# The FFN's bias as a matmul of three bf16 rows, in place of additions on GpSimd

## The chip, the cores and the metric

One core of a Trainium2 chip runs the whole program. The time is the device time of one execution in microseconds. The engines work side by side and wait for each other by semaphores: TensorE (PE, with PEld for its weight loads), VectorE (DVE), ScalarE (ACT), GpSimd (POOL) and SyncE (SP), which issues the DMAs.

## What is computed

x is 4 batches of 2048 rows of 256 values. The kernel computes a "macaron" block: half an FFN, attention, half an FFN.

```
ffn(x) = x @ W.T + b + (x @ V_r) @ C.T          # b: 256 values, V_r and C: rank 32
x = x + 0.5 * ffn(layernorm(x))
x = x + attn(layernorm(x))                      # 16 heads of 16, causal, polymax in place of softmax
x = x + 0.5 * ffn(layernorm(x))
```

`polymax` is x*x + 1 for positive scores and a straight line for negative ones, over 1000. The two FFNs have the same weights and the same bias.

## The kernel before

The 8192 rows are cut into 16 chunks of 512 (a chunk is 4 blocks of 128 rows). Each chunk goes through three stages: A (LayerNorm `ln1`, transposes `z1T`, first FFN `ffn`, LayerNorm `ln2`, transposes `z2T`), B (q, k, v, their splits into three bf16 parts, and a running state) and C (projection `proj`, LayerNorm `ln3`, transposes `z3T`, second FFN `out`). W and V_r C are folded into one matrix `w_ffn` at the start, already times 0.5.

Between them runs the attention, 16 iterations (4 batches by 4 groups of 4 heads) of 40 tiles, each tile in two halves. A half is two heads' scores: bf16 matmuls into the PSUM tile `score`, of which there are two. DVE or ACT raises them into `rp` (`L926`, `L831`); on tiles of the diagonal a mask is applied on POOL (`L710`) and a linear part `lin` is made; POOL and ACT square them (`L735`, `L847`, `L851`), and PE multiplies by v into `y_ps` three tiles later.

The order is written out by hand. A global list of slots says what every engine does; each engine walks the same slots in its own queue. A whole iteration has 80 slots, one half in each. The tables `A_FULL`, `B_FULL`, `C_FULL` put the stages' jobs into the slots: in a whole iteration `ffn` has slots 38 to 45 of a chunk's A stage, `out` slots 71 to 78 of another chunk's C stage. A job fills one of two PSUM banks (`bank`) in pieces, one piece a slot. A job of `ffn` or `out` has 4 pieces: two blocks of rows, and for each the two halves (`kc`) of the 256 inputs. Its chunk has two such jobs.

Every matmul is cut by `strips` into four of 32 columns of its stationary operand. They go to the four column groups of the array, run side by side, and are called a set below. An fp32 matmul leaves two records in the trace, a bf16 one leaves one. So a piece of `ffn` is 8 records of `bank<-w_ffn,zT`, and a set of scores is 4 records of `score<-qs,ks`.

The bias is added on POOL: `add_bias` runs in four slots behind the four of `normalise`, in place on the FFN's input x (`x_sb` for `ln1`, the tile `x2`, shown as `x`, for `ln3`), and its last part raises `xb_ready` or `x2b_ready`. DVE waits for that before it empties a bank with x = x + bank (`L897` for `ffn`, `L908` for `out`). DVE and POOL take everything in the order of their queues, so what stands behind a waiting instruction waits too.

Of the kernel before, what the change touches and what calls it, by code (L numbers as in the profile page):

```python
# [7 lines left out]
BF16 = mybir.dt.bfloat16  # L8
ALU = mybir.AluOpType
# [3 lines left out]
P = 128  # L13
BATCH, SEQ, DM = 4, 2048, 256
HEADS, HD = 16, 16
KC = DM // P
CH = 512
NB = CH // P
# [6 lines left out]
STRIP = 32  # L25
# [4 lines left out]
SPLITS = 3  # L30
# [83 lines left out]
C_LATE = {"proj": (0, 4), "ln3": 8, "z3T": (20, 21), "out": (22, 26)}  # L114
C_SHORT = {"proj": (0, 4), "ln3": 8, "z3T": (20, 21), "out": (22, 26)}

AGGR, SCALES, ROOT, NORM, BIAS = NB, NB + 4, NB + 2, NB + 5, 2 * NB + 5


@dataclass(eq=False)  # L120
# [17 lines left out]
class Order:  # L138
# [27 lines left out]
    def finish(self):  # L166
        self.jobs.sort(key=lambda x: x.start)
        ends = [x.start + PIECES[x.kind] for x in self.jobs]
        assert ends == sorted(ends)
        per = {"act": 0, "dve": 0}  # L170
        for k, x in enumerate(self.jobs):
            per[x.who] += 1
            x.k, x.emptied = k, per[x.who]
        self.place = {(x.kind, x.chunk, x.i): x for x in self.jobs}
        self.pieces, self.empties, self.steps = {}, {}, {}
        for x in self.jobs:
            for p in range(PIECES[x.kind]):
                self.pieces.setdefault(x.start + p, []).append((x, p))
            self.empties.setdefault(x.empty_at, []).append(x)
        for (kind, chunk), at in self.ln.items():  # L180
            for step in range(BIAS + NB):
                self.steps.setdefault(at + step, []).append((kind, chunk, step))

    def made(self, kind, chunk, i):
# [96 lines left out]
def build(nc, x_in, w_attn, w_proj, ffn_w, ffn_b, ffn_v, ffn_c, out):  # L281
    ctx = ExitStack()
    with ctx:
        def sb(name, shape, dt=F32):
            return ctx.enter_context(nc.sbuf_tensor(name, shape, dt))
# [4 lines left out]
        def sem(name):  # L290
            return ctx.enter_context(nc.semaphore(name))
# [14 lines left out]
        w_qkv = sb("w_qkv", [P, KC, 3 * DM])  # L306
        w_out = sb("w_out", [P, KC, DM])
        bias_half = sb("bias_half", [P, DM])
        smask = sb("smask", [QR, DM])
        slope_mask = sb("slope_mask", [P, 2, P])  # L310
        rise = sb("rise", [P, 1])
# [62 lines left out]
        x1_stored = sem("x1_stored")  # L374
# [3 lines left out]
        st_stored = sem("st_stored")  # L378
        c_loaded = sem("c_loaded")
        out_stored = sem("out_stored")  # L380
        xb_ready = sem("xb_ready")
        x2b_ready = sem("x2b_ready")
        stats_done = {k: sem(f"stats_{k}") for k in LNS}
        aggr_done = {k: sem(f"aggr_{k}") for k in LNS}
        var_done = {k: sem(f"var_done_{k}") for k in LNS}
# [3 lines left out]
        z_ready = {k: sem(f"z_ready_{k}") for k in LNS}  # L389
# [266 lines left out]
        def _(pool):  # L656
# [26 lines left out]
            pool.wait_ge(const_ready, 14)  # L683
            pool.tensor_scalar(bias_half[:], bias_half[:], 0.5, 0.0, ALU.mult, ALU.add).then_inc(const_ready, 1)
            pool.wait_ge(const_ready, CONSTS)

            def normalise(k, src, dst, chunk, i):
                if i == 0:
# [9 lines left out]
                                         ALU.mult, ALU.add)  # L698
                if i == NB - 1:
                    ins.then_inc(z_ready[k], 1)  # L700

            def add_bias(k, x, ready, chunk, i):
                if i == 0:
                    pool.wait_ge(z_ready[k], chunk + 1)
                ins = pool.tensor_tensor(x[:, i, :], x[:, i, :], bias_half[:], ALU.add)
                if i == NB - 1:
                    ins.then_inc(ready, 1)

            def mask(block, heads_in_it, fill=0.0):
                pool.affine_select(out=block, in_=block, compare_op=ALU.is_ge, fill=fill, base=0,  # L710
# [4 lines left out]
            def slot(s):  # L715
                H = o.halves.get(s)
                if H is not None and H % 2:
                    T = H // 2
                    off = TILES[T % NT][2]
                    buf = rp[T % RP_BUFS]  # L720
                    if is_diag(T) and shared(T):
                        wait_raised(pool, H)
                        mask(buf[:, 2:4, off:off + P], 2, -RISE)
                        wait_lin(pool, H)
                        mask(lin[diag_index(T) % L_BUFS][:, 2:4, :], 2)
                        wait_raised(pool, H - 1)
                        mask(buf[:, 0:2, off:off + P], 2)
                        pool.wait_ge(masked, o.masked[T] + 3)
                    elif is_diag(T):
                        wait_raised(pool, H)  # L730
                        mask(buf[:, :, off:off + P], QH)
                    if shared(T):
                        wait_raised(pool, H - 1)
                        half = buf[:, 0:2, off:CH]
                        pool.tensor_tensor(half, half, half, ALU.mult).then_inc(squared["pool"], 1)  # L735
                for k, chunk, step in o.steps.get(s, ()):
                    src, dst = {"ln1": (x_sb, z), "ln2": (x1, z), "ln3": (x2[chunk % 2], z3)}[k]
                    if 0 <= step - NORM < NB:
                        normalise(k, src, dst, chunk, step - NORM)
                    if 0 <= step - BIAS < NB and k != "ln2":  # L740
                        add_bias(k, src, xb_ready if k == "ln1" else x2b_ready, chunk, step - BIAS)
                for b, i, step in split_at.get(s, ()):
                    if b >= EARLY and step != 1:
                        split(pool, b, i, step)
                for x in o.empties.get(s - 1, ()):
                    if x.kind == "state":
                        b, i = x.chunk, x.i
                        wait_emptied(pool, "state", b, i)
                        if i == 0 and b > 0:
                            pool.wait_ge(st_stored, b * 16)  # L750
                        if i > 0 or b % CPB:
                            pool.wait_ge(st_added, b * NB + i)
                        add = st_add[i % 2][:].rearrange("r (h d) -> r h d", h=HEADS)
                        if i == 0 and b % CPB == 0:
                            if b == 0:
                                pool.wait_ge(st_zero, 16 * BATCH)
                            pool.tensor_copy(heads[:, 0], add).then_inc(st_added, 1)
                        else:
                            pool.tensor_tensor(heads[:, i], heads[:, (i - 1) % NB], add, ALU.add).then_inc(st_added, 1)
# [107 lines left out]
        def _(dve):  # L867
# [19 lines left out]
            def empty(x):  # L887
                kind, a, i, src = x.kind, x.chunk, x.i, bank[x.k % 2]
                done = emptied["dve"]
                two = src[:].rearrange("p (b d) -> p b d", b=2)  # L890
                dve.wait_ge(job_done, x.k + 1)
                if kind == "ffn":
                    if i == 0:
                        dve.wait_ge(xb_ready, a + 1)
                        if a > 0:
                            dve.wait_ge(x1_stored, a * 16)
                    nc.vector.tensor_tensor(x1[:, 2 * i:2 * i + 2, :], two, x_sb[:, 2 * i:2 * i + 2, :], ALU.add).then_inc(done, 1)  # L897
                if kind == "proj":
                    if i == 0:
                        dve.wait_ge(c_loaded, (a + 1) * 32)  # L900
                        if a > 1:
                            dve.wait_ge(out_stored, (a - 1) * 16)
                    nc.vector.scalar_tensor_tensor(x2[a % 2][:, 2 * i:2 * i + 2, :], two, 1.0 / DIVISOR, x1c[:, 2 * i:2 * i + 2, :],
                                                   ALU.mult, ALU.add).then_inc(done, 1)
                if kind == "out":
                    if i == 0:
                        dve.wait_ge(x2b_ready, a + 1)
                    nc.vector.tensor_tensor(x2[a % 2][:, 2 * i:2 * i + 2, :], two, x2[a % 2][:, 2 * i:2 * i + 2, :], ALU.add).then_inc(done, 1)  # L908
                if kind == "state":
                    if a * NB + i >= 2:  # L910
                        dve.wait_ge(st_added, a * NB + i - 1)
                    nc.vector.tensor_tensor(st_add[i % 2][:], src[0:QR, 0:DM], smask[:], ALU.mult).then_inc(done, 1)
# [76 lines left out]
        def _(pe):  # L989
# [30 lines left out]
            def job(x, piece):  # L1020
# [12 lines left out]
                if kind in ("ffn", "out", "proj", "v", "k"):  # L1033
                    if first and kind == "proj":
                        pe.wait_ge(c_loaded, (a + 1) * 32)
                    if first and kind in ("ffn", "out"):
                        wait_emptied(pe, {"ffn": "z1T", "out": "z3T"}[kind], a, 1)
                    w = {"ffn": w_ffn, "out": w_ffn, "proj": w_out, "v": w_qkv[:, :, 2 * DM:], "k": w_qkv[:, :, DM:2 * DM]}[kind]
                    src = {"ffn": zT, "out": z3T, "proj": y_c, "v": z2T, "k": z2T}[kind]
                    blk = 2 * i + piece // 2  # L1040
                    ins = strips(half, src[:, kc, P * blk:P * blk + P], w[:, kc, :], start=kc == 0, stop=kc == KC - 1)
                if kind == "qT":
                    if first:
                        wait_emptied(pe, "z2T", a, 1)
# [127 lines left out]
```

## Time and profile before

| | us |
|---|---|
| median of 3 runs | 1924.37 (1923.38 to 1930.8) |
| the profiled execution | 1931.65 |
| its span on the core | 1929.9 |
| PE busy in it | 1665.2 (86%) |
| DVE, ACT, POOL busy | 1361.7, 1363.2, 1326.5 (71%, 71%, 69%) |
| PE's mean granted clock | 0.965 of full |

Busy shares are means over the whole span. A busy PE is one with a matmul in its pipe, so that its idle time is understated; the start to the next start says how long it is really taken. Durations below come from the one profiled execution.

### The profile page before, as it was taken

How to read it: one execution, taken by the hardware profiler on the slowest of the kernel's cores; microseconds unless marked ns; L12 is line 12 of the kernel's file. 1: busy time of each engine (PE TensorE's matmuls, PEld its weight loads, DVE VectorE, ACT ScalarE, POOL GpSimd, SP SyncE). 2: the span in 40 equal slices, each digit the busy share in tenths (PEclk: the TensorE clock that was granted, in tenths of full speed). 3: DMA queues.
4: the chain of work that ended last, by engine and by line, in shares of the span. 5: the costliest groups of instructions: out<-in, count | busy, mean ns of one | idle time of the engine just before them, and what ended most of it. 6: DMA issues, size and time to landing. Idle time of an engine off the chain costs nothing.

```text
span 1929.9 us, 66983 instructions
## 1 busy us (share of the span) xinstructions
PE 1665.2 (86%) x27158; PEld 814.6 (42%) x27158; DVE 1361.7 (71%) x3313; ACT 1363.2 (71%) x2178; POOL 1326.5 (69%) x1419
## 2 busy tenths in 40 slices
PE   4677789898989989898998989898898999898785
PEld 2343334343444435353443535344444444443342
DVE  1465677777777867778786777878676778787672
ACT  1244568787888777777877877777787788888561
POOL 3344558787778868777676877867677767686552
PEclk8888889999999999999999999999999999999897
DMA  2344433241424233341523334241324222323111
GB/s 75 124 128 129 114 106 108 83 110 49 133 67 136 85 103 95 99 132 50 159 66 111 87 106 128 71 135 57 117 86 130 86 72 80 82 73 78 49 37 59
DMA packets 155191, 183.14 MB, mean 95 GB/s; under 512 B 22012, under 2 KB 129660, under 8 KB 152836
## 3 DMA queue, kind: packets, MB, share of 16 engines
q1 hardware_dynamic: 154884, 178.82, 31.6%
q8 instruction: 221, 3.62, 0.8%
q14 instruction: 86, 0.70, 0.1%
HBM read 102.43 MB, written 76.30 MB: 93 GB/s over the span
## 4 chain that ended last, share of the span: by engine, by line
PE 54%; DVE 15%; ACT 12%; issue 8%; POOL 8%; DMA 2%; SPq 0%; ACTq 0%; POOLq 0%; DVEq 0%
PE y_ps L991 20%; PE score L991 16%; PE bank L991 14%; DVE rp L926 9%; ACT rp L831 4%; ACT rp L851 3%; PE bank L1017 3%; POOL rp L735 2%; POOL z L697 2%; ACT rp L847 2%; DVE lin L932 2%; DMA part_scratch<-parts 1%; POOL rp L710 1%; POOL parts L465 1%; DMA x1c<-x_scratch 1%
## 5 line engine op out<-in xcount | busy, mean ns | idle before, releaser
L926 DVE TENSOR_SCALAR rp<-score 128x512 f32<-128x512 f32 (+2 forms) x1728 | 944.1, 573 | 276.0 <-PE score L991 271.3
L991 PE MATMUL score<-qs,ks 96*32 96x512 bf16 (+3 forms) x10240 | 742.7, 354 | 137.8 <-DVE rp L926 74.6
L735 POOL TENSOR_TENSOR rp<-rp 128x1024 f32<-128x1024 f32 (+1 forms) x416 | 756.3, 1830 | 125.1 <-DVE rp L926 114.1
L831 ACT ACTIVATE rp<-score 128x512 f32<-128x512 f32 (+1 forms) x832 | 458.4, 592 | 267.8 <-PE score L991 266.2
L991 PE MATMUL y_ps<-rp,vt 128*16 128x512 f32 (+3 forms) x5120 | 597.8, 537 | 24.3 <-ACT rp L851 13.3
L991 PEld LDWEIGHTS score<-qs,ks 96*32 96x32 bf16 x10240 | 294.4, 96 | 547.9 <-DVE rp L926 266.8
L847 ACT ACTIVATE rp<-rp,rise 128x1024 f32<-128x1024 f32 (+1 forms) x416 | 462.6, 1144 | 1.7 <-POOL rp L710 1.7
L710 POOL TENSOR_SCALAR_AFFINE_SELECT rp<-rp 128x256 f32<-128x256 f32 (+1 forms) x384 | 185.2, 484 | 317.2 <-DVE rp L926 161.5
L851 ACT ACTIVATE rp<-rp 128x1024 f32<-128x1024 f32 (+2 forms) x224 | 291.1, 1305 | 131.4 <-DVE rp L926 66.0
L932 DVE SCALAR_TENSOR_TENSOR lin<-score,slope_mask 128x128 f32<-128x128 f32 x768 | 214.4, 279 | 0.0
L991 PEld LDWEIGHTS y_ps<-rp,vt 128*16 128x16 f32 x5120 | 134.4, 97 | 111.5 <-ACT rp L851 25.7
L991 PE MATMUL bank<-w_ffn,zT 128*32 128x256 f32 x2048 | 160.3, 401 | 5.4 <-ACT zT L791 5.4
L991 PE MATMUL bank<-w_qkv,z2T 128*32 128x256 f32 x2048 | 152.5, 388 | 11.2 <-ACT parts L808 11.2
L1017 PE MATMUL bank<-ident,z 128*128 128x128 f32 x384 | 72.7, 327 | 45.2 <-POOL z L697 42.9
L991 PE MATMUL y_ps<-lin,vt 128*16 128x128 f32 x2048 | 106.2, 276 | 0.0
L991 PEld LDWEIGHTS bank<-w_ffn,zT 128*32 128x32 f32 x2048 | 69.0, 115 | 79.6 <-issue 51.6
L697 POOL TENSOR_SCALAR z<-x,rstd_ln,shift_ln 128x256 f32<-128x256 f32 x128 | 72.6, 575 | 40.8 <-DVE shift_ln L885 39.3
L991 PEld LDWEIGHTS y_ps<-lin,vt 128*16 128x16 f32 x2048 | 61.5, 97 | 80.0 <-issue 67.8
L991 PEld LDWEIGHTS bank<-w_qkv,z2T 128*32 128x32 f32 x2048 | 67.3, 112 | 62.4 <-issue 28.0
L991 PE MATMUL bank<-w_out,y_c 128*32 128x256 f32 x1024 | 83.4, 400 | 11.8 <-DMA x1c<-x_scratch 11.8
L1017 PEld LDWEIGHTS bank<-ident,z 128*128 128x128 f32 x384 | 49.6, 164 | 88.5 <-issue 78.2
L697 POOL TENSOR_SCALAR z<-x_sb,rstd_ln,shift_ln 128x256 f32<-128x256 f32 x64 | 35.0, 558 | 68.2 <-DVE shift_ln L885 68.2
(78 smaller groups left out, 1360.0 us busy)
## 6 DMA issues: line engine op xcount, KB each, us to landing
part_scratch<-parts SPq DMA_DIRECT2D x16, 1536.0 KB, 7.5
qs<-part_scratch SPq DMA_DIRECT2D x384, 64.0 KB
ks<-part_scratch SPq DMA_DIRECT2D x384, 64.0 KB, 2.4
state_scratch<-st_new SPq DMA_DIRECT2D x16, 528.0 KB
st<-state_scratch SPq DMA_DIRECT2D x64, 132.0 KB
x_sb<-in_L_attn_x_dram SPq DMA_DIRECT2D x16, 512.0 KB, 4.4
x_scratch<-x SPq DMA_DIRECT2D x16, 512.0 KB, 5.4
qT_scratch<-qkT SPq DMA_DIRECT2D x16, 512.0 KB, 3.8
```

The source lines that it names most:

```text
L465: ins = eng.tensor_tensor(parts[:, i, 2, :], rest[:], parts[:, i, 1, :], ALU.subtract)
L697: ins = pool.tensor_scalar(dst[:, i, :], src[:, i, :], rstd[k][:, i:i + 1], shift[k][:, i:i + 1], ALU.mult, ALU.add)
L710: pool.affine_select(out=block, in_=block, compare_op=ALU.is_ge, fill=fill, base=0, pattern=[[0, heads_in_it], [1, P]], channel_multiplier ...
L735: pool.tensor_tensor(half, half, half, ALU.mult).then_inc(squared["pool"], 1)
L831: nc.scalar.activation(rp[T % RP_BUFS][:, 2 + v, off:CH], score[H % S_BUFS][:, v, off:CH], ACT.Relu).then_inc(raised["act"], 1)
L847: nc.scalar.activation(part, part, ACT.Square, bias=rise[:]).then_inc(squared["act"], 1)
L851: nc.scalar.activation(whole, whole, ACT.Square).then_inc(squared["act"], 1)
L926: nc.vector.tensor_scalar(rp[T % RP_BUFS][:, 2 * u + v, off:CH], score[H % S_BUFS][:, v, off:CH], 0.0, RISE, ALU.max, ALU.add).then_inc(ra ...
L932: nc.vector.scalar_tensor_tensor(lin[D % L_BUFS][:, 2 * u + v, :], score[H % S_BUFS][:, v, off:off + P], ONE / SLOPE, slope_mask[:, 0, :], ...
L991: return nc.tensor.matmul(*args, start=start, stop=stop, skip_group_check=True)
L1017: ins = nc.tensor.transpose(dst[:, P * blk:P * blk + P], src[:, blk, P * i:P * i + P], ident[:])
```

## The change

The bias (times 0.5) is cut once, on POOL at the start, into three bf16 parts, each the rest that the last left over. They are put in rows 0, 32 and 64 of `bias_rows`, a tile of 96 rows of zeros otherwise. Each half of a bank in a job of `ffn` or `out` now begins with one more set: `ones` (96 x 128, bf16) as the stationary operand, `bias_rows` (96 x 256, bf16) as the moving one, and `w_ffn` is added to that. `add_bias` is gone, with its two semaphores and DVE's waits for them.

```
-AGGR, SCALES, ROOT, NORM, BIAS = NB, NB + 4, NB + 2, NB + 5, 2 * NB + 5
+AGGR, SCALES, ROOT, NORM = NB, NB + 4, NB + 2, NB + 5
...
             pool.wait_ge(const_ready, CONSTS)
+            pool.memset(bias_rows[:], 0.0).then_inc(bias_step, 1)
+            pool.memset(ones[:], 1.0).then_inc(bias_step, 1)
+            pool.tensor_copy(bias_parts[:, 0, :], bias_half[:]).then_inc(bias_step, 1)
+            pool.wait_ge(bias_step, 3)
+            pool.tensor_tensor(bias_half[:], bias_half[:], bias_parts[:, 0, :], ALU.subtract).then_inc(bias_step, 1)
+            pool.wait_ge(bias_step, 4)
+            pool.tensor_copy(bias_parts[:, 1, :], bias_half[:]).then_inc(bias_step, 1)
+            pool.wait_ge(bias_step, 5)
+            pool.tensor_tensor(bias_parts[:, 2, :], bias_half[:], bias_parts[:, 1, :], ALU.subtract).then_inc(bias_step, 1)
+            pool.wait_ge(bias_step, 6)
+            for s in range(SPLITS):
+                row = slice(STRIP * s, STRIP * s + 1)
+                pool.tensor_copy(bias_rows[row, :], bias_parts[row, s, :]).then_inc(bias_step, 1)
+                pool.wait_ge(bias_step, 7 + s)
...
-            def add_bias(k, x, ready, chunk, i):
-                if i == 0:
-                    pool.wait_ge(z_ready[k], chunk + 1)
-                ins = pool.tensor_tensor(x[:, i, :], x[:, i, :], bias_half[:], ALU.add)
-                if i == NB - 1:
-                    ins.then_inc(ready, 1)
...
-                    if 0 <= step - BIAS < NB and k != "ln2":
-                        add_bias(k, src, xb_ready if k == "ln1" else x2b_ready, chunk, step - BIAS)
...
                 if kind == "ffn":
-                    if i == 0:
-                        dve.wait_ge(xb_ready, a + 1)
-                        if a > 0:
-                            dve.wait_ge(x1_stored, a * 16)
+                    if i == 0 and a > 0:
+                        dve.wait_ge(x1_stored, a * 16)
...
                 if kind == "out":
-                    if i == 0:
-                        dve.wait_ge(x2b_ready, a + 1)
...
+                    if first and kind == "ffn" and a == 0:
+                        pe.wait_ge(bias_step, 6 + SPLITS)
...
-                    ins = strips(half, src[:, kc, P * blk:P * blk + P], w[:, kc, :], start=kc == 0, stop=kc == KC - 1)
+                    biased = kind in ("ffn", "out")
+                    if biased and kc == 0:
+                        strips(half, ones[:], bias_rows[:], start=True, stop=False)
+                    ins = strips(half, src[:, kc, P * blk:P * blk + P], w[:, kc, :], start=kc == 0 and not biased,
+                                 stop=kc == KC - 1)
```

On PE, before, in slots 38 to 41 of an iteration, where the first `ffn` job of chunk 9 fills `bank0` (a row of x4 is a set of strips, of x8 two sets):

```order
L991 MATMUL y_ps0<-rp1,vt 16x512 x4
L991 MATMUL bank0<-w_ffn,zT 32x256 x4
L991 MATMUL score1<-qs,ks 32x512 x8
L991 MATMUL bank0<-w_ffn,zT 32x256 x4
L991 MATMUL score0<-qs,ks 32x256 x8
L991 MATMUL y_ps0<-rp2,vt 16x384 x4
L991 MATMUL y_ps0<-lin3,vt 16x128 x4
L991 MATMUL bank0<-w_ffn,zT 32x256 x4
L991 MATMUL score1<-qs,ks 32x256 x8
L991 MATMUL bank0<-w_ffn,zT 32x256 x4
```

On PE, now, at the same place:

```order
L995 MATMUL y_ps0<-rp1,vt 16x512 x4
L995 MATMUL bank0<-bias_rows,ones 32x256 x4
L995 MATMUL bank0<-w_ffn,zT 32x256 x4
L995 MATMUL score1<-qs,ks 32x512 x8
L995 MATMUL bank0<-w_ffn,zT 32x256 x4
L995 MATMUL score0<-qs,ks 32x256 x8
L995 MATMUL y_ps0<-rp2,vt 16x384 x4
L995 MATMUL y_ps0<-lin3,vt 16x128 x4
L995 MATMUL bank0<-bias_rows,ones 32x256 x4
L995 MATMUL bank0<-w_ffn,zT 32x256 x4
L995 MATMUL score1<-qs,ks 32x256 x8
L995 MATMUL bank0<-w_ffn,zT 32x256 x4
```

Each job has a new set ahead of its first and of its third piece, so ahead of the scores of the slots behind them; nothing else is moved.

On POOL, before, in the slots of `ln1`'s normalisation and bias in a whole iteration (`z` are the normalised rows, `rp` the tiles of the attention):

```order
L697 TENSOR_SCALAR z<-x_sb,rstd_ln,shift_ln 128x256 x2
L710 AFFINE_SELECT rp<-rp 128x4x128
L697 TENSOR_SCALAR z<-x_sb,rstd_ln,shift_ln 128x256 x2
L705 TENSOR_TENSOR x_sb<-x_sb,bias_half 128x256 x2
L710 AFFINE_SELECT rp<-rp 128x4x128
L705 TENSOR_TENSOR x_sb<-x_sb,bias_half 128x256 x2
L735 TENSOR_TENSOR rp<-rp 128x1024 x2
L710 AFFINE_SELECT rp<-rp 128x2x128
```

On POOL, now, at the same place:

```order
L714 TENSOR_SCALAR z<-x_sb,rstd_ln,shift_ln 128x256 x2
L720 AFFINE_SELECT rp<-rp 128x4x128
L714 TENSOR_SCALAR z<-x_sb,rstd_ln,shift_ln 128x256 x2
L720 AFFINE_SELECT rp<-rp 128x4x128
L745 TENSOR_TENSOR rp<-rp 128x1024 x2
L720 AFFINE_SELECT rp<-rp 128x2x128
```

A mask and two squarings lose the four additions that stood ahead of them in POOL's queue.

## Rows read from the trace of the kernel before

**Rows 1.** The page: the chain that ended last, by engine and by line.

```profile
PE 54%; DVE 15%; ACT 12%; issue 8%; POOL 8%; DMA 2%; SPq 0%; ACTq 0%; POOLq 0%; DVEq 0%
PE y_ps L991 20%; PE score L991 16%; PE bank L991 14%; DVE rp L926 9%; ACT rp L831 4%; ACT rp L851 3%; PE bank L1017 3%; POOL rp L735 2%; POOL z L697 2%; ACT rp L847 2%; DVE lin L932 2%; DMA part_scratch<-parts 1%; POOL rp L710 1%; POOL parts L465 1%; DMA x1c<-x_scratch 1%
```

**Rows 2.** Who waited for whom: us in total, times, longest.

```profile
PE score L991 <- DVE rp L926: 74.6, 150, 2.5
PE score L991 <- DVE lin L932: 52.8, 93, 2.2
...
PE y_ps L991 <- POOL rp L735: 3.7, 8, 0.8
```

**Rows 3.** The same view for ACT.

```profile
ACT rp L851 <- POOL rp L710: 65.4, 30, 2.8
```

**Rows 4.** The page's costliest groups: busy, mean ns | idle before.

```profile
L991 PE MATMUL bank<-w_ffn,zT 128*32 128x256 f32 x2048 | 160.3, 401 | 5.4 <-ACT zT L791 5.4
```

**Rows 5.** Tile `w_ffn`: duration ns min/median/max, first and last start.

```profile
L991 PE MATMUL bank<-w_ffn,zT x2048: 376/379/636, 27.4 to 1921.5; 128*32 128x256 f32 x187
```

**Rows 6.** The chain in order of time, 626 to 631: start, us, what.

```profile
628.35 0.43 PE bank L991 x8
628.78 0.22 PE score L991 x8
```

**Rows 7.** PE's timeline at the same place: start, us, what.

```profile
628.59 0.41 PE L991 MATMUL score<-qs,ks 96*32 96x256 bf16 x8
```

**Rows 8.** Tile `w_ffn` in three windows: PE, PEld and ACT busy, clock, DMA.

```profile
0.00:300.00 300.00, 31.81 (x384) 14.82 (x384) 0.77 (x2) 0.87 0.37 113
300.00:1890.00 1590.00, 119.01 (x1536) 48.77 (x1536) 0.00 (x0) 0.99 0.32 92
1890.00:1929.90 39.90, 9.47 (x128) 5.46 (x128) 0.00 (x0) 0.75 0.20 58
```

**Rows 9.** The chain through chunk 9's `ffn`, 653 to 663.

```profile
654.22 0.43 PE bank L991 x8
...
656.71 0.43 PE bank L991 x8
...
662.11 0.43 PE bank L991 x8
```

**Rows 10.** PE's timeline there: the piece that the chain passes by.

```profile
658.90 0.63 PE L991 MATMUL bank<-w_ffn,zT 128*32 128x256 f32 x8
```

**Rows 11.** PE's timeline through an `out`, 693 to 712: [idle before <-releaser].

```profile
701.98 0.63 PE L991 MATMUL bank<-w_ffn,zT 128*32 128x256 f32 x8
...
703.66 1.05 PE L991 MATMUL y_ps<-rp,vt 128*16 128x512 f32 x8 [0.61 <-ACT rp L851]
...
707.99 0.62 PE L991 MATMUL bank<-w_ffn,zT 128*32 128x256 f32 x8
709.15 0.40 PE L991 MATMUL score<-qs,ks 96*32 96x512 bf16 x4 [0.54 <-DVE rp L926]
```

**Rows 12.** Tile `bias_half`: the additions, duration ns min/median/max.

```profile
L705 POOL TENSOR_TENSOR x_sb<-x_sb,bias_half x64: 720/732/742, 24.7 to 1306.2; 128x256 f32<-128x256 f32 x64
L705 POOL TENSOR_TENSOR x<-x,bias_half x64: 719/727/751, 664.2 to 1915.3; 128x256 f32<-128x256 f32 x64
```

**Rows 13.** POOL's timeline behind an `ln1`, 857 to 867.

```profile
858.56 1.42 POOL L705 TENSOR_TENSOR x_sb<-x_sb,bias_half 128x256 f32<-128x256 f32 x2
...
861.94 3.75 POOL L735 TENSOR_TENSOR rp<-rp 128x1024 f32<-128x1024 f32 x2
```

**Rows 14.** POOL's timeline, 1008 to 1013.

```profile
1008.29 3.75 POOL L735 TENSOR_TENSOR rp<-rp 128x1024 f32<-128x1024 f32 x2
```

**Rows 15.** DVE's timeline, 1008 to 1013.

```profile
1009.12 2.93 DVE L885 SCALAR_TENSOR_TENSOR shift_ln<-mv_ln,rstd_ln 128x4 f32<-128x4 f32 x1
```

**Rows 16.** POOL's first work behind the constants, at the start.

```profile
22.40 2.17 POOL L697 TENSOR_SCALAR z<-x_sb,rstd_ln,shift_ln 128x256 f32<-128x256 f32 x4 [10.19 <-DVE shift_ln L885]
```

**Rows 17.** DVE at the end: the first half of the last `out`.

```profile
1919.78 0.69 DVE L908 TENSOR_TENSOR x<-bank,x 128x512 f32<-128x512 f32 x1 [8.84 <-PE bank L991]
```

More of the change, by code:

```diff
@@ L180, in finish @@
         for (kind, chunk), at in self.ln.items():
-            for step in range(BIAS + NB):
+            for step in range(NORM + NB):
                 self.steps.setdefault(at + step, []).append((kind, chunk, step))
@@ L308, in build @@
         bias_half = sb("bias_half", [P, DM])
+        bias_parts = sb("bias_parts", [P, SPLITS, DM], BF16)
+        bias_rows = sb("bias_rows", [STRIP * SPLITS, DM], BF16)
+        ones = sb("ones", [STRIP * SPLITS, P], BF16)
         smask = sb("smask", [QR, DM])
@@ L380, in build @@
         out_stored = sem("out_stored")
-        xb_ready = sem("xb_ready")
-        x2b_ready = sem("x2b_ready")
+        bias_step = sem("bias_step")
         stats_done = {k: sem(f"stats_{k}") for k in LNS}
```

## The prediction

> **What bounds the kernel now.** I read the chain of work that ended last first [rows 1]: 54% of it is PE, 15% DVE, 12% ACT and only 8% POOL, and its largest lines are matmuls, those into the banks at 14% among them. The additions of the bias are in no piece of it: I went through it in order of time, and POOL stands there with masks, squarings, splits and `z`, never with `L705`. Then the waits [rows 2]: PE waits for DVE to empty a score tile, 74.6 and 52.8 us, and for POOL's squares only 3.7 us. So PE's own work is most of the path, and the rest is the round trip of the scores PE, DVE or ACT, PE. What matters for this change is how a slot with a piece of `ffn` or `out` goes: whether PE is the last there or waits a moment later anyway.
>
> **What is removed.** POOL loses 64 additions of 732 ns and 64 of 727 ns [rows 12], 93.4 us of its 1326.5. DVE loses 32 waits that appear nowhere as the last of its waits. By the chain this is worth nothing. The place where it could count is behind `ln1`: there POOL works without a gap from the addition at 858.56 to the end of two squarings at 865.69 [rows 13], and these will come up to 2.9 us (4 x 0.73) sooner. But the chain stays on PE through that stretch, and PE's whole waiting for squares is 3.7 us [rows 2]. I take 0, with 3.7 us as the near bound of a gain and the rival below for a larger one.
>
> **What is added at the start.** Nine small POOL instructions, the largest over 128x256 like the additions. Even at 0.73 us each they are 6.6 us, and POOL stands idle for 10.19 us before its first `z` at 22.40, where the chain comes by way of ACT and DVE [rows 16]. PE needs the rows only at 27.4 [rows 5]. I take 0. Without that cover it would cost 6.6 us, once.
>
> **What is added on PE.** Four sets a chunk and stage (two jobs, two halves of a bank), so 16 x 2 x 4 = 128 sets, 512 matmuls of 256 bf16 columns.
>
> The price of a set: the same shape is there in the scores. Two sets of 256 bf16 columns (8 records) take 0.22 us of the chain, one fp32 set of 256 columns 0.43 us [rows 6], and the timeline says that these 8 scores are indeed the 256-column ones [rows 7]. So a bf16 set is 0.11 us, or a quarter of 0.43, 0.108 us. The scores stand between fp32 sets on both sides there, so the change of type costs nothing that shows, and neither do their weight loads. I take 0.108: 128 x 0.108 = 13.8 us at full clock.
>
> Some run at the half clock, 1.2 GHz. Records of `w_ffn` last 379 ns in the median, 636 at most [rows 5] and 401 in the mean [rows 4]; with only two levels the share of slow ones is (401-379)/(636-379) = 0.086. The term becomes 13.8 x 1.086 = 15.0 us of PE time.
>
> A page of the Trainium skill speaks against the change here: "TensorE: Matmul & The Clock Gate", Part 3 (Packing small matmuls), says that a weight load overlaps with running matmuls only where the row group differs, and here all four strips have the same rows. With its figure of a column per 1/1.2 ns, four loads of 32 columns would be an estimated 0.107 us, and the set would cost double. By that the sum would be near 30 us of PE time. The trace disagrees, in sets of this very form: eight loads and eight matmuls in 0.22 us [rows 6].
>
> **How much of it lies on the path.** In a whole iteration I laid the pieces beside the chain. Chunk 9's `ffn` has eight pieces in eight slots; new sets come before the first, third, fifth and seventh. The chain goes through the first, third and seventh (654.22, 656.71 and 662.11 [rows 9]) and passes by the fifth (658.90 [rows 10]), which runs while the path is on DVE. So 3 of 4. In an `out`, the first piece (701.98) is followed by a wait of 0.61 us for ACT and the fifth (707.99) by one of 0.54 us for DVE [rows 11]: a set of 0.108 goes into those for nothing. The third and seventh lie on the chain. So 2 of 4. Together 0.625 of the sets. This is the cover: if the waits behind them were gone, all would count.
>
> This pattern holds from 300 to 1890, with 119.0 of the 160.3 us of `w_ffn` [rows 8]. The other 41.3 us (0.26) are in the opening, where stages run alone, and at the end, where PE works through the last two `out` jobs' chunks, partly at the half clock, and DVE waits for it 8.84 us [rows 17]; matching pieces and chain there gives about 0.9. Together 0.74 x 0.625 + 0.26 x 0.9 = 0.70. Matching all pieces from 27.4 to 1921.5 against the chain gives the same, 0.70.
>
> **Sum.** 15.0 x 0.70 = +10.5 us, minus 0. The profiled execution took 1931.65, so it would take 1942.1. That execution stands 7.3 us (0.4%) above the median; the difference carries over, and the median 1924.37 becomes **1934.9 us**.
>
> **Rivals.**
>
> *Hidden.* The chain is one path; beside it PE waits 127.4 us for DVE [rows 2], and the sets could slide more into these waits than I counted, while POOL's relief gives back a little of its 3.7. At a share of 0.35 and 1 us back: 5.3 - 1 = +4.3, 1928.7. For it: all waits behind `out`'s first and fifth pieces are five times a set's length. Against: in the slots of the third and seventh pieces PE goes through without a stop.
>
> *POOL's relief decides: faster.* Behind `ln1` and `ln3` POOL's masks and squarings come sooner; ACT waits 65.4 us in 30 places for a mask [rows 3]. If a third of that (22 us) and the 3.7 us vanished, the sum would be 10.5 - 25.7 = -15, so 1909. It decides from about 0.16 us gained on the path for each of the 128 additions (20 us in all). Against: the chain has none of them, and where it is on POOL no addition stands ahead in that stretch.
>
> Beside it stands "GPSIMD Engine Reference" of the Trainium skill, section 1 (Specifications): GpSimd shares its way into SBUF with VectorE, with contention where a DVE instruction has two SBUF inputs. The trace agrees: `shift_ln`, four values a partition, lasts 2.93 us beside POOL's squarings [rows 14, 15]. What that would give here is nothing, since these small instructions of DVE stand in slots without additions; what they lose, they lose to `L735`. It raises the chance of this rival little.
>
> *Sets that are not hidden: slower still.* If a set cost its loads too, 0.10 more, or if the change from ones to `w_ffn` in the same bank made PE wait, the sum would be 128 x 0.208 x 1.086 x 0.70 = 20.2, so 1944.6. Against it: [rows 6].
>
> **How the numbers follow.** Forecast as worked out 0.62, its own range 1931 to 1939 (shares of 0.5 and 1 of the 15.0 us, with a little of POOL's relief off the lower). Hidden 0.22, POOL decides 0.06, loads not hidden 0.10. The range leaves out the 0.06, about half of the 0.10 and a part of the hidden case below 1926: 1926 to 1942. 0.5% of 1924.37 is 9.6 us, about what a measurement of this kernel can tell from no change. The forecast is only 0.9 us above that bound, so I split it: 0.22 of the 0.62 within, 0.40 above. Slower 0.40 + 0.10 = 0.50; same 0.22 + 0.22 = 0.44; faster 0.06.
>
> **What would show it.** Right: 512 records of `bank<-bias_rows,ones`; 8 of them in the chain (or from start to start) at 0.22 us; scores behind a job's third and seventh pieces come 0.11 us later and stay late; an iteration with both stages is 5 x 0.108 = 0.54 us longer; the last `out` takes 4 x 0.216 = 0.86 us more at the half clock; POOL's busy time falls by about 90 us with nobody the faster for it. Wrong: a gap or a weight load that stands alone before `w_ffn`'s first set (loads not hidden); iterations of the same length though PE has more to do (hidden); ACT's wait for masks much below 65.4 us and shorter iterations (POOL decides); another granted clock in the opening, which would move some us either way and is no part of my sum.

## The result, and the profile after

| | before | after |
|---|---|---|
| median, us (13 runs each) | 1927.98 | 1932.23 |
| the profiled execution | 1931.65 | 1936.32 |
| its span | 1929.9 | 1934.6 |
| POOL busy | 1326.5 | 1240.8 |
| PE's mean granted clock in it | 0.965 | 0.967 |

The ratio is 1.0034, with a 95% interval from 1.0021 to 1.0046: the change costs 6.6 us (4.0 to 8.9). It is not the ratio of the two medians, which lie 4.3 us apart, and one of the 13 runs of before, of 2334.04 us, is left out of it. The forecast was +10.5 us, so the sign was right, the time lies in the range, and the size is two thirds of what was forecast, or less by the medians.

Part of the near hit on the time itself is luck: 1934.9 was built on 1924.37, the median of three runs, and the median of the thirteen is 3.6 us higher. And the largest chance, 0.50, had gone to a slowdown of more than 0.5%; the measured one is 0.34%.

First the chain of the changed kernel, by engine and by line, to be held against [rows 1].

```profile
PE 55%; DVE 15%; ACT 12%; issue 8%; POOL 7%; DMA 2%; SPq 0%; ACTq 0%; POOLq 0%; DVEq 0%
PE y_ps L995 20%; PE score L995 16%; PE bank L995 15%; DVE rp L930 9%; ACT rp L839 4%; ACT rp L859 3%; PE bank L1021 3%; ACT rp L855 2%; POOL z L714 2%; POOL rp L745 2%; DVE lin L936 1%; DMA x1c<-x_scratch 1%; DMA part_scratch<-parts 1%; POOL rp L720 1%; POOL parts L468 1%
```

PE's matmuls into the banks went from 14% to 15%, and the order of the large lines stayed. These shares don't show the change: in a second profile of the changed kernel the banks have 14% again, and in a second one of the kernel before POOL has 5% where it had 8. Then the new set in the view of its tile (duration min/median/max, first and last start):

```profile
L995 PEld LDWEIGHTS bank<-bias_rows,ones x512: 92/94/151, 27.2 to 1925.2; 96*32 96x32 bf16 x171
L995 PE MATMUL bank<-bias_rows,ones x512: 269/273/421, 27.2 to 1925.5; 96*32 96x256 bf16 x171
```

273 ns is the time of one record through the pipe and not what a set takes from PE. That is read from start to start, or in the chain, here through chunk 9's `ffn`, the place of [rows 9]:

```profile
655.40 0.55 PE bank L995 x12
...
657.90 0.55 PE bank L995 x12
658.45 0.22 PE score L995 x8
658.67 0.48 PE bank L995 x8
...
663.43 0.55 PE bank L995 x12
```

A piece of `ffn` with a set of the bias has 12 records and 0.55 us, where it had 8 and 0.43: the set takes 0.11 to 0.12 us. Three of the four are in the chain, the first, third and seventh piece, as before. And this is PE's timeline at an `out`, the place of [rows 11], with the idle time before each in brackets:

```profile
701.95 0.29 PE L995 MATMUL bank<-bias_rows,ones 96*32 96x256 bf16 x4
...
703.63 1.05 PE L995 MATMUL y_ps<-rp,vt 128*16 128x512 f32 x8 [0.52 <-ACT rp L859]
...
708.07 0.29 PE L995 MATMUL bank<-bias_rows,ones 96*32 96x256 bf16 x4
...
709.23 0.40 PE L995 MATMUL score<-qs,ks 96*32 96x512 bf16 x4 [0.43 <-DVE rp L930]
```

The waits behind the two sets were 0.61 and 0.54 us and are 0.52 and 0.43. The sets went into them whole.

The waits of PE and ACT on POOL (us, times, longest), to be held against [rows 2, 3]:

```profile
PE y_ps L995 <- POOL rp L745: 2.5, 6, 0.7
```

```profile
ACT rp L859 <- DVE rp L930: 86.7, 39, 5.7
ACT rp L859 <- POOL rp L720: 45.9, 23, 2.8
```

Against [rows 3], ACT waits 19.5 us less for POOL's masks, and 20.7 us more for DVE. That looks like POOL's relief handed on to DVE, and it isn't. These are the same two waits in the first profile of before (its DVE line alone), in its second, unedited one, and in the second of the changed kernel:

```profile
ACT rp L851 <- DVE rp L926: 66.0, 32, 5.7
...
ACT rp L851 <- DVE rp L926: 82.3, 38, 5.7
ACT rp L851 <- POOL rp L710: 48.1, 24, 2.8
...
ACT rp L859 <- DVE rp L930: 71.9, 34, 5.7
ACT rp L859 <- POOL rp L720: 59.6, 28, 2.8
```

The sum of both is 130.4 to 132.6 us in all four, and how it is split moves by 14 to 17 us between two profiles of one and the same kernel. So 65.4 us was no fixed figure of the kernel before, and its fall says nothing of POOL.

POOL at the start, where the wait of 10.19 us was [rows 16]: nine instructions from 12.06 to 16.17, and `z` 0.2 us sooner than before.

```profile
12.06 0.31 POOL L689 MEMSET bias_rows<- 96x256 bf16 x1
...
14.88 1.29 POOL L701 COPY bias_rows<-bias_parts 1x256 bf16<-1x256 bf16 x3
22.20 2.17 POOL L714 TENSOR_SCALAR z<-x_sb,rstd_ln,shift_ln 128x256 f32<-128x256 f32 x4 [6.02 <-DVE shift_ln L893]
```

What the forecast did not have is seen when the whole iterations with both stages are laid side by side. I take as the mark of an iteration the start of `z1T`, the transposes behind `ln1`, just ahead of `ffn` (PE, `bank<-ident,z`), which lie in the same slot of each. In the windows view the columns are the stretch and its length, busy time of PE, PEld, DVE, ACT and POOL, PE's granted clock, DMA share, GB/s. Two of the six iterations of before, from 646.5 to 1315.5 us:

```profile
646.50:758.60 112.10, 101.03 (x1700) 49.89 (x1696) 83.70 (x204) 85.22 (x138) 84.63 (x91) 0.98 0.34 101
...
870.60:981.10 110.50, 99.41 (x1701) 48.81 (x1697) 84.03 (x204) 85.11 (x138) 84.94 (x91) 1.00 0.37 102
```

Two of the six of the changed kernel:

```profile
647.70:758.80 111.10, 100.30 (x1733) 49.95 (x1729) 83.54 (x204) 85.14 (x138) 79.00 (x83) 1.00 0.35 102
...
1202.70:1315.30 112.60, 101.79 (x1733) 50.33 (x1729) 83.86 (x204) 85.21 (x138) 79.33 (x83) 0.98 0.36 100
```

There are two lengths in each kernel, and the clock tells them apart. Before: 110.4 to 110.5 us at full clock (two iterations), 112.0 with the clock at 1.2 GHz in one place (four). After: 110.8 to 111.2 (five) and 112.6 (one). At like clock an iteration became 0.5 to 0.6 us longer on the mean, where the forecast had 5 x 0.108 = 0.54. But the sum over the six went from 669.0 to 667.6 us, since three falls of the clock at 1.6 us each were gone.

### The profile page after: what moved, and what is told of

Same layout as the page of the kernel before. It is cut to its first block, busy times and chain, and to the rows that moved or that the text cites. A ratio compares the mean times of both kernels' runs of the same rounds, so it can differ in the third digit from the quotient of the medians.

```text
span 1934.6 us, 67871 instructions
## 1 busy us (share of the span) xinstructions
PE 1672.3 (86%) x27670; PEld 825.5 (43%) x27670; DVE 1360.9 (70%) x3313; ACT 1363.2 (70%) x2178; POOL 1240.8 (64%) x1300
## 4 chain that ended last, share of the span: by engine, by line
PE 55%; DVE 15%; ACT 12%; issue 8%; POOL 7%; DMA 2%; SPq 0%; ACTq 0%; POOLq 0%; DVEq 0%
PE y_ps L995 20%; PE score L995 16%; PE bank L995 15%; DVE rp L930 9%; ACT rp L839 4%; ACT rp L859 3%; PE bank L1021 3%; ACT rp L855 2%; POOL z L714 2%; POOL rp L745 2%; DVE lin L936 1%; DMA x1c<-x_scratch 1%; DMA part_scratch<-parts 1%; POOL rp L720 1%; POOL parts L468 1%
## 5 line engine op out<-in xcount | busy, mean ns | idle before, releaser
L859 ACT ACTIVATE rp<-rp 128x1024 f32<-128x1024 f32 (+2 forms) x224 | 291.1, 1305 | 132.6 <-DVE rp L930 86.7
L845 ACT ACTIVATE lin<-score 128x128 f32<-128x128 f32 x256 | 76.2, 298 | 0.0
```

What stands on the lines that cost most here:

```text
L845: nc.scalar.activation(lin[D % L_BUFS][:, 2 + v, :], score[H % S_BUFS][:, v, off:off + P], ACT.Copy, scale=SLOPE, bias=ONE).then_inc(lin_d ...
L859: nc.scalar.activation(whole, whole, ACT.Square).then_inc(squared["act"], 1)
```

## The experiments

Theory 1: the sets cost what was forecast and POOL's relief is worth nothing; what is missing is the clock. Theory 2: POOL's relief gave back about 4 us. Theory 3, beside the first: the sets themselves keep the clock up.

All times of experiments are compared with runs of before on the same chip. There were two series, on two chips; the changed kernel's 13 runs belong to neither. Its ratio in the table is that to its own 13 runs of before, whose clocks aren't on record, and for the last two columns its runs are set against the first series. That comparison across series is the weak one: between the two series the kernel before differs by 2.6 us in the median. Since the clock differs from run to run, two more numbers are given where there are many runs: the mean of the runs' granted clocks, and the difference to before at equal clock. For that a straight line was put through time against clock over all runs of a series, with one slope for all kernels (-1.24 us for each 0.001 of clock in the first series, -1.26 in the second; the runs' clocks are rounded to 0.001, which makes such a slope a little too flat).

The ± is two standard errors.

| kernel | runs | median, us | ratio (95%) | mean clock | at equal clock, us |
|---|---|---|---|---|---|
| before, first series | 25 | 1928.13 | 1 | 0.9667 | 0 |
| changed | 13 | 1932.23 | 1.0034 (1.0021 to 1.0046) | 0.9692 | +7.6 ± 1.5 |
| both | 12 | 1929.37 | 1.0010 (0.9999 to 1.0020) | 0.9696 | +6.3 ± 1.6 |
| none | 11 | 1928.49 | 1.0000 (0.9988 to 1.0012) | 0.9669 | +0.7 ± 1.4 |
| double | 4 | 1951.45 | 1.0118 (1.0104 to 1.0133) | 0.9660 | +21.5 ± 2.2 |
| wide | 8 | 1932.91 | 1.0025 (1.0014 to 1.0036) | 0.9669 | +5.3 ± 1.6 |
| before, second series | 23 | 1925.51 | 1 | 0.9680 | 0 |
| out wide | 12 | 1927.50 | 1.0007 (0.9993 to 1.0020) | 0.9690 | +2.1 ± 1.7 |
| ffn only | 12 | 1930.89 | 1.0019 (1.0001 to 1.0036) | 0.9682 | +4.5 ± 1.6 |

**Both: the additions stay, the sets come as well.**

```
+            pool.memset(bias_rows[:], 0.0).then_inc(bias_step, 1)
+            pool.memset(ones[:], 1.0).then_inc(bias_step, 1)
...
+                    if biased and kc == 0:
+                        strips(half, ones[:], bias_rows[:], start=True, stop=False)
```

> The additions stay on POOL and PE makes the new sets as well, with rows of zeros in them (the result is the reference's). PE's work is that of the changed kernel, POOL's that of before. Theory 1 (the sets are paid on the path, POOL's relief is worth nothing, and what is missing of the forecast is the clock, which fell in fewer iterations): an iteration with both stages and full clock is 111.0 us as in the changed kernel, against 110.4 before, and the time is that of the changed kernel within 2 us, a ratio of 1.003 to 1.004. Theory 2 (POOL's relief gave back about 4 us of 10.5): the full 10.5 us come out, a ratio of 1.0055, and iterations longer than the changed kernel's by about 0.3 us.

Measured: 1.0010, below the 1.003 of theory 1 too, and +6.3 us at equal clock, the changed kernel's +7.6 within the error. Theory 2 wanted 10.5 us and longer iterations than the changed kernel's. In the profiled execution every iteration had a fall of the clock, so that there is none at full clock to read; one of the six:

```profile
646.60:759.10 112.50, 101.70 (x1732) 50.43 (x1728) 83.53 (x204) 85.01 (x138) 84.44 (x91) 0.98 0.35 101
```

112.5 us against the 112.6 of the changed kernel's iteration with a fall, with POOL at 84.4 us in place of 79.3. With the same clock, 5 us more of POOL's work make no iteration longer. The mean clock of its runs is the highest of the table, and only the fit, by way of that clock, brings the time to theory 1. The profiled execution took 1942.24 us and the unprofiled ones 1927.2 to 1933.9.

**None: the bias is left out.** The additions and DVE's waits for them are taken out of the kernel before, and no set comes in.

```
-                    if 0 <= step - BIAS < NB and k != "ln2":
-                        add_bias(k, src, xb_ready if k == "ln1" else x2b_ready, chunk, step - BIAS)
```

> The bias is left out altogether: no additions on POOL, no sets on PE. What is left is POOL's relief alone. Theory 1 (no relief): iterations of 110.4 us at full clock, the clock falls in as many as before, ratio 1.000 within 0.001. Theory 2 (relief of 4 us): ratio 0.998 and iterations of about 110.1 us.

Measured: 1.0000, +0.7 ± 1.4 us. Two iterations of it:

```profile
872.20:982.80 110.60, 99.53 (x1700) 49.36 (x1696) 83.70 (x204) 85.06 (x138) 79.36 (x83) 1.00 0.35 102
1207.00:1317.40 110.40, 99.36 (x1701) 48.75 (x1697) 83.96 (x204) 85.06 (x138) 79.36 (x83) 1.00 0.35 103
```

The length of before to 0.2 us, with 5.5 us less of POOL's work in each, and a fall of the clock in the other four, as before. This measures the relief of POOL, and DVE's missing waits, by themselves: nothing, and by the fit's error at most 0.7 us of gain.

**Double: each set twice, the second with rows of zeros.**

```
+                        strips(half, ones[:], zero_rows[:], start=False, stop=False)
```

> The changed kernel with a second set, of zero rows, behind each set of the bias: 256 sets in place of 128 (the result is the reference's). Theory 1: an iteration with both stages grows from 111.0 to 111.5 us at full clock (five of its eight sets on the path, 0.108 each), and the whole by up to 10.5 us over the changed kernel where the clock's falls are as many: ratio to before 1.008 to 1.009. If sets after the first slide into waits (the hidden rival), 111.2 us and 1.006. Theory 3 (sets keep the clock up, so they partly pay for themselves): at most one iteration between 640 and 1320 us with a fall of the clock.

Measured: 1.0118, above every expectation. Iterations at full clock are as forecast by theory 1:

```profile
760.70:872.10 111.40, 100.81 (x1764) 50.35 (x1761) 83.73 (x204) 85.05 (x138) 79.33 (x83) 1.00 0.36 102
1098.20:1209.70 111.50, 100.89 (x1764) 50.57 (x1760) 83.33 (x204) 85.13 (x138) 79.02 (x83) 1.00 0.36 102
985.10:1098.20 113.10, 102.75 (x1764) 51.45 (x1760) 83.62 (x204) 85.24 (x138) 79.42 (x83) 0.98 0.35 100
```

Four of the six had a fall, so more work in sets does not by itself keep the clock up: theory 3's expectation missed. At equal clock the second 128 sets cost 13.9 us (21.5 less 7.6), or 0.109 us each. That would be nearly the whole of them, where 0.7 had been on the path of the first. In the profiled executions (1947.63 against 1936.32 us, both at a clock of 0.967) it is 11.3 us. Only three runs of this kernel are unprofiled, and the 7.6 comes from another series. Behind the opening the profile has 6.6 us for the second 100 sets (the table further down), 0.6 of them on the path, as the iterations say. Where the rest of the 13.9 comes from stays open. Against the hidden rival: second sets lengthen an iteration nearly as the first did, by 0.4 to 0.5 us.

**Wide: one set of 512 columns ahead of a job's first piece.**

```
-                    if biased and kc == 0:
-                        strips(half, ones[:], bias_rows[:], start=True, stop=False)
+                    if biased and piece == 0:
+                        strips(dst, ones[:], bias_rows[:].rearrange("r b d -> r (b d)"), start=True, stop=False)
```

> The bias of both halves of a bank in one set of 512 columns ahead of a job's first piece, in place of a set of 256 ahead of the first and of the third. PE's work is the same. By the place of the pieces in the chain (out: first and fifth piece are followed by waits of 0.61 and 0.54 us; ffn: the fifth is passed by), only the set ahead of the first piece of ffn, 0.216 us, stays on the path of an iteration, in place of 5 x 0.108: iterations of 110.6 to 110.7 us at full clock in place of 111.0, and 4 to 5 us less than the changed kernel, ratio to before about 1.001. If it makes no difference where the sets stand: 111.0 us and 1.0035.

```profile
641.70:752.20 110.50, 99.89 (x1716) 49.13 (x1712) 82.47 (x204) 85.03 (x138) 78.98 (x83) 1.00 0.35 102
752.20:862.90 110.70, 100.09 (x1716) 49.25 (x1712) 83.72 (x204) 85.06 (x138) 79.36 (x83) 1.00 0.37 102
975.10:1087.70 112.60, 101.78 (x1717) 50.26 (x1713) 83.63 (x204) 85.20 (x138) 79.42 (x83) 0.98 0.34 101
```

The iterations at full clock are 110.5 to 110.7 us, as expected from where the waits stand. The time is not: 1.0025 against an expected 1.001, and +5.3 against the changed kernel's +7.6 us at equal clock. Where the sets stand matters in the iterations. Of the saving of 4 to 5 us only 2.3 ± 1.9 come out at equal clock; the ratios, 1.0034 and 1.0025, differ by less still, and the mean clock was 0.9669 against 0.9692. In the one profile of this kernel the whole behind the opening, estimated without the clock, is 3.5 us shorter than the changed kernel's (the table further down). So the profile has most of the saving, and the times don't show it.

**Before and changed once more,** unedited, for a second profile of each.

> The kernel before, once more, for a second profile of it. If the lengths of the iterations are the kernel's own and the rest is the clock, those at full clock are 110.4 us again and those with one fall of the clock 112.0, whichever they are; the number of falls between 640 and 1320 us may differ from the four of the first profile. If POOL or the queues vary from run to run, other lengths appear.

Measured 1924.79 us at a clock of 0.968. The six lengths are 112.0, 110.4, 112.5, 112.1, 111.9 and 110.4. Those at full clock are the same to a tenth; with a fall there is a 112.5 among the 112.0. Four falls again.

> The changed kernel once more. Iterations at full clock of 110.9 to 111.1 us, those with a fall of 112.4 to 112.6. If the sets themselves keep the clock up, at most one fall between 640 and 1320 us again; if that was chance, any number, up to every iteration, as in the kernel with both.

Measured 1937.45 us, and a fall in every one of the six iterations, 112.4 to 112.7 us. Two of them:

```profile
757.80:870.20 112.40, 101.71 (x1732) 50.61 (x1728) 83.77 (x204) 85.03 (x138) 79.25 (x83) 0.98 0.34 101
870.20:982.70 112.50, 101.92 (x1733) 51.52 (x1729) 83.86 (x204) 85.15 (x138) 79.34 (x83) 0.98 0.34 101
```

So the same kernel has had one fall and six. The difference of the first pair of profiles in the iterations, 669.0 to 667.6 us, would have been 669.3 to 675.5 in the second: the sign of such a comparison hangs on the falls.

**Out wide and ffn only: one of the two biases over PE.** The one has `biased = kind == "out"` and the set of 512 columns, and POOL adds the bias behind `ln1` alone; the other has `biased = kind == "ffn"` and the sets of the change, and POOL adds behind `ln3` alone.

> Only the bias of out goes over PE, as one set of 512 columns ahead of a job's first piece; that of ffn stays on POOL. Theory 1: both sets of a stage go into the waits of 0.61 and 0.54 us that stand there, so an iteration with both stages and full clock is 110.4 us, that of before; only the last stages at the end pay, 1 to 3 us in all at equal clock. If the waits don't cover them, 110.4 + 0.43 = 110.8 us and 5 us or more in all.

```profile
644.70:755.10 110.40, 99.83 (x1709) 49.97 (x1705) 83.62 (x204) 85.04 (x138) 81.67 (x87) 1.00 0.35 103
867.00:977.40 110.40, 99.82 (x1709) 49.18 (x1705) 83.98 (x204) 85.07 (x138) 82.01 (x87) 1.00 0.35 102
```

110.4 us, the length of before, and at `out` PE's timeline shows why:

```profile
698.51 0.39 PE L1009 MATMUL bank<-bias_rows,ones 96*32 96x512 bf16 x4
...
700.19 1.05 PE L1009 MATMUL y_ps<-rp,vt 128*16 128x512 f32 x8 [0.42 <-ACT rp L871]
...
704.51 0.40 PE L1009 MATMUL bank<-bias_rows,ones 96*32 96x512 bf16 x4
...
705.67 0.40 PE L1009 MATMUL score<-qs,ks 96*32 96x512 bf16 x4 [0.33 <-DVE rp L944]
```

The waits of 0.61 and 0.54 us are 0.42 and 0.33: 0.2 us of each is filled, and the sets are free. What is left, +2.1 ± 1.7 us at equal clock, agrees with 1 to 3 us for the last stages, and the ratio 1.0007 is no difference.

> Only the bias of ffn goes over PE, as in the changed kernel, and that of out stays on POOL. Theory 1: three of four sets on the path of an iteration, 110.4 + 0.32 = 110.75 us at full clock, and at equal clock 6 us over before: 0.12 x (24 sets of the opening x 0.9 + 40 x 0.75). If POOL's additions behind ln1, which stand ahead of masks and squarings without a gap, had cost something, less than that: 110.4 to 110.6.

```profile
647.10:758.00 110.90, 99.84 (x1716) 49.90 (x1713) 83.51 (x204) 85.12 (x138) 81.72 (x87) 1.00 0.35 102
758.00:868.60 110.60, 99.88 (x1716) 49.58 (x1712) 83.84 (x204) 85.13 (x138) 82.06 (x87) 1.00 0.35 102
...
1205.20:1316.00 110.80, 99.80 (x1717) 49.68 (x1713) 83.81 (x204) 85.20 (x138) 82.17 (x87) 1.00 0.36 102
```

110.6 to 110.9 us, where 110.75 was expected, and +4.5 ± 1.6 us in all, where 6 was. The mean of the three iterations, 110.8, leaves no gain from POOL behind `ln1`, where its queue had been the fullest; the shortest alone would have allowed some.

## Why the forecast was right, and its size too large

*POOL's relief is worth nothing:* right, and shown by leaving the additions out (1.0000) and by adding the sets with the additions kept. POOL's busy time fell by 85.7 us, where about 90 had been forecast. The rival in which POOL decides is out, and so is the near bound of 3.7 us. The wait of ACT for masks, which the forecast named as a sign, can't tell: it was 65.4 and 48.1 us in the two profiles of the kernel before, and 71.1 us in that of the wide sets, which has no additions.

*The preparation at the start is free:* right; it took 4.1 us of a wait of 10.19.

*A set costs 0.108 us, with its loads and the change of type hidden:* right, 0.11 to 0.12 in the chain. The rule of the Trainium skill's page "TensorE: Matmul & The Clock Gate", Part 3, that loads overlap only across row groups, would have made it an estimated 0.2, and the trace disagrees here too.

*Five of eight sets of an iteration on the path:* right piece for piece. 110.4 became 111.0 us. `out` alone with its sets in the waits stays at 110.4, `ffn` alone is at 110.6 to 110.9, and the wide sets are at 110.5 to 110.7. That decides against the hidden rival, whose +4.3 us the plain difference of the medians would fit as well: its sign was iterations of the same length.

*The opening and the end at 0.9:* not shown. In the first pair of profiles the mark in the second whole iteration came 0.65 us later (437.60 and 438.25), with the clock of the first 300 us at 0.87 and 0.88. In the second pair it came 2.6 us later (433.2 and 435.8), and in the kernel without any bias at 439.2, later than in all four. The 28 sets ahead of that mark can't be read from single profiles.

The stretch from the last mark to the end grew by 4.9 us (614.40 to 619.32), and by 3.4 in the second pair (611.7 to 615.1). From the last `out`'s first matmul to DVE's last half it went from 5.87 to 6.23 us (1916.08 to 1921.95, and 1920.44 to 1926.67): 0.36 us and not the 0.86 of the forecast. Its four sets took 0.17, 0.22, 0.22 and 0.12 us from start to start, 0.73 in all; the half clock ended ahead of the fourth, and sooner in the `w_ffn` matmuls than before. The four sets of the `out` ahead of it cost PE nothing, since it then waits 6 to 7 us for the last load from `x1`. The forecast had counted them.

That wait grew by 1.1 us (6.08 to 7.16), and this is a cost of the change that no term had. The load is issued behind four stores of `y` on SP, here before and now:

```profile
1891.66 1.73 SPq L549 DMA_DIRECT2D y_scratch<-y_sb  x4
...
1894.97 2.88 SPq L552 DMA_DIRECT2D y_scratch<-y_sb  x4
```

In all six profiles of kernels with sets in `out` the four stores take 2.6 to 2.9 us, in all four without them 1.73. In five of the six it is the second issue that lasts 1.3 to 1.6 us in place of 0.42. Why is not shown.

DVE's end of the wait for the first half of the last `out`, to be held against [rows 17]:

```profile
1924.53 0.69 DVE L912 TENSOR_TENSOR x<-bank,x 128x512 f32<-128x512 f32 x1 [9.22 <-PE bank L995]
```

8.84 became 9.22: two sets, 0.17 and 0.22 us, are in it.

*The step that was off* is the one that carried the clock over as it was. The forecast took a share of 0.086 of slow records from the trace and multiplied by 1.086; it named another clock in the opening as a thing outside its sum, and took it for granted that the whole iterations have theirs. They don't. At equal clock the change costs 7.6 ± 1.5 us by the fit. By the first pair of profiles it is +4.7 us of span with three falls fewer in the whole iterations, so 4.7 + 4.8 = 9.5; by the second it is +12.7 us with two falls more, so 12.7 - 3.2 = 9.5 again. That the clock made the difference in the profiled pairs is shown, by the lengths of the iterations. For the 6.6 us of the unprofiled runs it is not: the clocks of the 13 runs of before aren't on record. Against the first series, at a mean clock of 0.9692 to 0.9667, the difference of the means is 4.6 us, and the step from there to 7.6 rests on the fit.

The traces allow one more reading. Behind the mark at 437 us, where 100 of the 128 sets are, I count each microsecond at half clock as half of one. This is an estimate; for a fall, 3.4 us at half clock that cost 1.6, it holds.

| profile | behind the mark, us | of it at half clock | estimate at full clock |
|---|---|---|---|
| before, twice | 1492.3, 1489.8 | 60.6, 54.6 | 1462.0, 1462.5 |
| none | 1492.8 | 61.1 | 1462.3 |
| changed, twice | 1496.3, 1499.9 | 54.3, 61.1 | 1469.2, 1469.3 |
| both | 1503.3 | 71.4 | 1467.6 |
| double | 1508.4 | 65.1 | 1475.8 |
| wide | 1494.7 | 57.7 | 1465.8 |
| out wide, ffn only | 1492.9, 1492.6 | 57.6, 57.3 | 1464.1, 1463.9 |

Two profiles of one kernel agree to 0.5 us here, where their times lie 6.9 us apart (before) and 1.1 (changed). For the kernel with both it gives 5.1 to 5.6 us over before, with the most time at half clock of all, so it may be off by a microsecond or two. The change costs 6.7 to 7.3 us behind the mark, some 1.1 of it the longer stores. 100 sets at 0.108 are 10.8 us, so the sets are on the path with 0.5 to 0.6, near the 0.625 that the forecast has for whole iterations. Its 0.70 for all 128 sets is neither shown nor refuted, since the opening can't be read: the same estimate for the opening scatters from 397.9 to 405.3 us, whatever the kernel.

*Why the clock was higher on the mean* is not settled. That the sets keep it up by giving PE more to do is unlikely: with twice the sets the mean was 0.966, and the changed kernel itself has had six falls of six. How often each pattern comes is not known.

No kernel here beats the one before. Leaving out all work of the bias gives 1.0000, so at most 0.7 us is to be had from it.

## What to carry to other kernels

Ask of work that is moved off an engine whether that engine is ever in the chain behind it; 86 us taken from POOL's busy time were worth nothing, and a kernel with the work left out shows that, once it has enough runs to see past the clock. On the engine that bounds, a new piece costs its start-to-start time only where no wait follows: lay it ahead of an instruction that waits anyway, and it is free up to the length of the wait. And where a loop's iterations come in two lengths, sort them by granted clock before two kernels are compared; the difference of like iterations agreed with the forecast to 0.1 us where the totals of one kernel scattered by 9. Take a second profile of the unchanged kernel before a shift between two waits is put down to the change: here it moved by up to 17 us from one to the next.

## What the hardware showed

The fall of the clock in a whole iteration comes at one place in it or not at all. Before it PE had waited 0.69, 0.20 and 1.54 us for DVE within some 5 us, in iterations with the fall and in those without: the same records, the same waits. This is PE's timeline of before in the iteration from 646.5, with the fall:

```profile
687.18 0.40 PE L991 MATMUL score<-qs,ks 96*32 96x512 bf16 x4 [1.54 <-DVE rp L926]
...
688.00 1.69 PE L991 MATMUL y_ps<-rp,vt 128*16 128x512 f32 x8
```

and in the iteration from 870.6, without:

```profile
911.25 0.40 PE L991 MATMUL score<-qs,ks 96*32 96x512 bf16 x4 [1.54 <-DVE rp L926]
...
912.07 1.05 PE L991 MATMUL y_ps<-rp,vt 128*16 128x512 f32 x8
```

The granted clock from 688 to 692 was 0.57 on the mean, at 1.2 GHz for most of it, against 1.00 from 912 to 916. One fall costs the iteration 1.6 us.

The falls can repeat. In the kernel before, iterations with a fall last 111.9 to 112.5 us and four of six have it, in both profiles. In the changed kernel and in the one with both, an iteration with a fall lasts 112.4 to 112.7 us, and in two of their three profiles all six have it, in the third only the last. The other profiles have three falls of six (wide, out wide, ffn only) or four (none, double). Whether the added work changes this pattern is not shown: there are two profiles each of the kernel before and the changed one and one each of the others, and no cause is shown either.
